# One core, two layers with gathered weights: ring blocks 2 to 7 of the first pair issued behind x, ScalarE's table loaded first, the transposes of hw in two parts, the gathers of B in four later pairs

## The reference, cut to what matters

```
def layer0(x, ids):                      # first half of the kernel
    c    = einsum('bsi,boi->bso', x, weight[ids])        # 1024x1024 adapter of each sequence
    h    = c @ lora_A.T                                  # 8 experts x rank 16
    w    = top-2 of softmax(c @ W_router.T), renormalised
    lora = 2 * sum over experts of w * (h @ lora_B.T)
    return c @ W_base.T + b_base + lora
def layer1(x, ids):                      # second half
    y = per-sequence 64x64 mix of x by weights[ids]
    return y with features permuted, 16 heads of up (64->256), gelu, down (256->64), unpermuted
x = x + layer0(x, ids);  x = x + layer1(x, ids)
```

## Time and profile before

| | |
|---|---|
| median of three runs | 613.79 us (613.06 to 614.24) |
| the profiled execution, its own time | 612.9 us |
| its span | 611.1 us, so 1.8 us lie around it |
| TensorE busy in the span | 592.6 us (97%) |
| VectorE busy | 471.5 us (77%) |
| ScalarE, GpSimd busy | 144.6 and 127.1 us |
| first phase, 18 to 276 us | TensorE busy all but 4 us of it |
| second phase, 276 to 611 us | TensorE busy 330.26 of 335 us |
| granted TensorE clock | 1.00 in every stretch |

### The profile page before, as it was taken

The page is one execution under the profiler, slowest core; times in us unless marked ns, Lnnn a source line. Parts: engine busy times, 40 slices in busy tenths (PEclk is TensorE's granted clock), DMA queues, the critical chain, the costliest instruction groups (busy, mean ns, idle before and its releaser), DMA issues.

```text
span 611.1 us, 13485 instructions
## 1 busy us (share of the span) xinstructions
PE 592.6 (97%) x4375; PEld 348.2 (57%) x4376; DVE 471.5 (77%) x1303; ACT 144.6 (24%) x290; POOL 127.1 (21%) x194
## 2 busy tenths in 40 slices
PE   4999999999998999999999999999999999999996
PEld 3344444344433444457777676767676767676762
DVE  3068778878887779698888897779987889887862
ACT  2100000200020002153332524225332235232334
POOL 4010002121111220060022222222231313131312
PEclk9999999999999999999999999999999999999999
DMA  7999889899899997120023222222222222222222
GB/s 269 409 388 316 306 307 305 308 308 315 297 409 403 352 316 254 44 69 28 19 63 94 70 90 68 88 73 88 70 86 69 88 67 94 69 86 67 88 71 86
DMA packets 43428, 106.90 MB, mean 175 GB/s; under 512 B 8451, under 2 KB 17667, under 8 KB 43395
## 3 DMA queue, kind: packets, MB, share of 16 engines
q1 hardware_dynamic: 30914, 76.04, 35.7%
q0 software_dynamic: 6784, 21.51, 10.6%
q10 hardware_dynamic: 5696, 8.95, 4.2%
HBM read 98.09 MB, written 8.39 MB: 174 GB/s over the span
## 4 chain that ended last, share of the span: by engine, by line
PE 86%; DVE 6%; DMA 4%; issue 2%; ACTq 0%; SPq 0%; POOL 0%; DVEq 0%; another core or an unknown queue 0%; POOLq 0%
PE wide L536 26%; PE bank L643 20%; PE bank L651 10%; PE bank L731 8%; PE wide L714 8%; PE y_wide L567 4%; DVE c_pair L1096 3%; DMA ring<-adapters_dram 3%; PE y_wide L689 3%; PE wide L551 2%; DMA x_in<-x_seq_dram 1%; PE bank L663 1%; PE bank L664 1%; PE bank L667 1%; PE bank L743 1%
## 5 line engine op out<-in xcount | busy, mean ns | idle before, releaser
L536 PE MATMUL wide<-ring,x_in 128*64 128x512 f32 x960 | 209.6, 592 | 2.4 <-DMA ring<-adapters_dram 2.4
L536 PEld LDWEIGHTS wide<-ring,x_in 128*64 128x64 f32 x960 | 73.1, 137 | 127.1 <-issue 127.1
L1288 DVE STREAM_TRANSPOSE x_tok<-xres 32x128 f32<-32x128 f32 x464 | 140.2, 302 | 6.0
L1096 DVE STREAM_TRANSPOSE c_pair<-wide 32x256 f32<-32x256 f32 x240 | 107.1, 446 | 39.4 <-issue 21.7
L943 ACT ACTIVATE act_sb<-wide 128x512 f32<-128x512 f32 x120 | 66.5, 610 | 191.3 <-PE wide L714 191.3
L643 PE MATMUL bank<-c_hi,base_t 128*128 128x512 f32 x384 | 102.3, 390 | 0.0
L424 POOL DMA_INDIRECT xres<-xT_dram,row_in x32 | 35.0, 1094 | 230.8 <-DVE out_sb L1278 227.6
L643 PEld LDWEIGHTS bank<-c_hi,base_t 128*128 128x128 f32 x384 | 71.9, 188 | 15.3
L651 PE MATMUL bank<-c_lo,base_t 128*128 (+1 forms) x256 | 78.0, 390 | 0.0
L462 POOL COPY c_all<-c_pair 128x512 f32 x30 | 19.3, 669 | 213.9 <-DVE c_pair L1096 213.9
L858 ACT ACTIVATE small<-small 128x1 f32<-128x1 f32 x16 | 3.2, 203 | 217.3 <-DVE small L1132 217.3
(11 more groups left out here) (161 smaller groups left out, 601.5 us busy)
## 6 DMA issues: line engine op xcount, KB each, us to landing
ring<-adapters_dram SPq DMA_DIRECT2D x128, 512.0 KB, 5.8
x_in<-x_seq_dram ACTq DMA_DIRECT2D x32, 256.0 KB, 4.8
down_sb<-down_dram SPq DMA_DIRECT2D x32, 128.0 KB
up_raw<-up_dram SPq DMA_DIRECT2D x62, 64.0 KB
ar_sb<-lora_a_router_dram ACTq DMA_DIRECT2D x1, 544.0 KB, 4.3
mix_sb<-mix_dram SPq DMA_DIRECT2D x32, 16.0 KB, 2.0
xres<-xT_dram,row_in POOLq DMA_INDIRECT x32, 3.5
out_dram<-out_sb,row_out POOLq DMA_INDIRECT x28, 3.0
```

Of the source, the lines that this page charges most:

```text
L536: last = pe.matmul(acc[half][h][z * TOK:(z + 1) * TOK, :], x_in[:, half, z, k, :], ring[:, k, z, h * HALF:(h + 1) * HALF], start=(k == 0), ...
L1096: last = nc.vector.transpose(c_pair[r * SQ:(r + 1) * SQ, :, q * SQ:(q + 1) * SQ], wide[half][q * SQ:(q + 1) * SQ, :, :] .rearrange("p h (k ...
L1288: last = nc.vector.transpose(x1_tok[q * SQ:(q + 1) * SQ, :].rearrange("p (c f) -> p c f", f=P)[:, :, f * SQ:(f + 1) * SQ], xres[f * SQ:(f ...
```

## The change

Four edits. In `first_pair` SyncE waits, ahead of block 2, until both transfers of x for pair 0 have landed. ScalarE, after it has issued its first two transfers, waits for `ident` and copies one column of it, so that its table comes in there. `turn_four` is cut: after `route` of the third pair of a batch VectorE does the 4 transposes of row block 0 of `hw`, and in the fourth pair the other 12. The gathers of B and bias go from one each in t = 4 to 11 to two each in t = 10, 11, 12 and 13 (b_rows, bias, b_rows, bias).

```
-GATHERS = range(PAIRS // 4, PAIRS // 4 + KT)
+GATHERS = {PAIRS - 6 + n: (2 * n, 2 * n + 1) for n in range(KT // 2)}
...
                 for k in range(KT):
+                    if k == 2:
+                        sp.wait_ge(x_in_in[0], 32)
                     sp.dma_start(ring[:, k, 0, :], ...)
...
-                if t in GATHERS:
-                    j = t - GATHERS[0]
+                for j in GATHERS.get(t, ()):
                     gather(b_rows[:, j, :], lora_b, perm_sb[:, j:j + 1], b_in)
                     gather(bias[:, j:j + 1], bias_rows, perm_sb[:, j:j + 1], bias_in)
...
             act.sem_inc(hw_placed, 8)
+            act.wait_ge(ident_ok, 2)
+            nc.scalar.copy(th, ident[:, 0:1])
             act.wait_ge(lists_ok, 1)
...
-            def turn_four(i):
+            def turn_four(i, qs):
-                dve.wait_ge(hw_ok, i * 4 + 4)
-                dve.wait_ge(hw_placed, i * 8 + 8)
-                for q in range(P // SQ):
+                if qs[0] == 0:
+                    dve.wait_ge(hw_ok, i * 4 + 4)
+                    dve.wait_ge(hw_placed, i * 8 + 8)
+                for q in qs:
...
-                last.then_inc(hw_turned_ok, 1)
+                if qs[-1] == P // SQ - 1:
+                    last.then_inc(hw_turned_ok, 1)
...
                     else:
-                        turn_four(i)
+                        turn_four(i, range(1, 4))
                     route(t, hw_four[:, (n + 1) % 4, :])
+                    if n == 2:
+                        turn_four(i, range(0, 1))
```

## The result

The changed kernel takes 614.99 us (median of 16 runs, 614.47 to 617.45), the kernel before 612.24 us beside it (16 runs, 611.07 to 614.24). The ratio is 1.0046 with a 95% interval of 1.0035 to 1.0056: some 2.8 us slower. The forecast said 2.1 us slower; its 615.9 was built on the earlier median of 613.79, so the sum is what can be compared. The profiled execution has a span of 613.1 us and its own time is 614.93 (before: 611.1 and 612.9); the granted clock is 0.999.

A forecast was written before the change was run, and what follows sets the result against it. TensorE is 97% busy, so only first-phase holes can move. Terms: -0.2 (x) - 0.63 (hole at t = 4) - 0.3 (ring) + 1.8 (t = 10) + 1.4 (t = 12) = +2.1 us on 613.79, giving 615.9; range 612.6 to 617.8.

The forecast's parts named there:

- the copy goes from 203.48 to 206.4: Pair 10: four gathers hold the router's signal, VectorE's copy comes late, and the next router stalls 1.8 us.
- t = 12, 1.4: Pair 12: the copy waits for the fourth gather, 2.15 us later, and the router due at 246.99 stalls 1.4 us.
- t = 13: free: Pair 13: its router starts on the spot, so the four gathers there cost nothing.
- Not t = 12 but t = 13: Rival, 0.18: router 12 escapes, router 13 is caught on the end-setting chain; 2.8 us in place of 1.4, 617.3 us.
- the rival of the slipping signal: Rival, 0.24: the signal slips out between gathers, t = 10 and 12 cost nothing; sum -1.0 us, 612.8 us.
- hw in two parts: Moving 4 of 16 transposes ahead of `turn_pair(4)` closes TensorE's hole at 119.04: 0.63 us gained.
- The gathers' going would close it too: Gathers leaving t = 4 would alone close the 0.63 us hole before router 5; not additive with the split.
- x: Start, SyncE's wait before block 2: x lands at 17.6, block 2 at 21.4; 0.2 us gained, bounds 0.5 gained, 1.9 lost.
- after block 2 the ring keeps up: Pair 0: issues 0.62 us apart and 1.3 us per block against 1.72 of matmuls, so no further waits.
- Ring bytes, -0.3: Ring-bound stretch, 163 to 190 us: two 64 KB gathers of t = 8 and 9 go, gaining 0.3 us.
- Table, 0: Start: ScalarE's table first removes TensorE's 1.13 us wait at 13.59, but nothing follows from it; 0 gained.
- two engines that share nothing but the sender: First phase: VectorE and SyncE both get TensorE's signals late during gathers; used as evidence against a port lock.

The follow-up runs named there:

- e1: The changed kernel without SyncE's wait for x: 614.29 us, ratio 1.0028.
- e2: The changed kernel with the gathers of B and bias back at t = 4 to 11, one each: 613.46 us, ratio 1.0024.
- e3: The kernel before with only the gathers moved to t = 10 to 13, two each: 612.85 us, ratio 1.0002.
- f2: The kernel before with ScalarE's table first and the gathers at t = 10 to 13, no wait for x, no split: 611.12 us, ratio 0.9983.
- e6: The kernel before with split, table first, and the old gathers waiting until VectorE has copied the router's result: 611.43 us, ratio 0.9983.
- e7: The changed kernel with the two-and-two gathers one pair earlier, at t = 9 to 12: 615.11 us, ratio 1.0031.
- e8: The changed kernel with four bias gathers each at t = 10 and 12, four b_rows gathers each at t = 11 and 13: 612.66 us, one run.
- e5: The kernel before with hw's transposes split and ScalarE's table first, old gathers, no wait for x: 613.08 us, ratio 1.0011.
- e4: The kernel before with SyncE's wait for x alone: 613.34 us, ratio 1.0024.
- f3: The kernel before with ScalarE's table first and nothing else: 612.21 us, ratio 0.9995.
- f4: The kernel before again, no edit, profiled once more: 612.94 us, one run.
- f1: The kernel before with one edit, GpSimd's gathers of B and bias waiting for VectorE's gap_ok of their pair: 611.82 us, ratio 0.9982.

## Why the prediction was right, and where its steps failed

**Sign and size: right; the mechanism behind them: right; its place: wrong.** The forecast was a loss because TensorE's signal is held while GpSimd issues several gathers in a row. e1, e2, e3 and f2 show that: the changed kernel with the old places has no such loss, and e6, with the same gathers behind the copy, has no late router's signal at all. But the step "the copy goes from 203.48 to 206.4", with its stall of 1.8 us at t = 10, failed, and so did "t = 12, 1.4". The copies came 2.1 us (t = 10), 1.7 (t = 11) and, where caught, 2.9 and 3.2 (t = 12 in f2, e7) after their router; they did not wait for the whole run, and the pair's slack took them in. (SyncE's ring issues did wait for it: 1.14 to 1.17 after the last gather, near the 0.95 of the forecast. But they had slack for it.) And the step "t = 13: free" failed the other way: 4.6 us late in the changed kernel and in e1, all of 2.8 us on the chain.

**The rival came true in its second half.** "Not t = 12 but t = 13" had the mechanism (`turn_pair(12)` behind row block 0 begins late, router 12 starts on the spot and escapes, router 13 is caught, `turn_pair(14)` at 257.0; it was 256.30) and the price: 2.8. What it also had, 1.8 at t = 10, was nothing, as in the rival of the slipping signal. Each rival held for some pairs. I had given 0.18 to the one and 0.24 to the other and none to both together. That the total came out near is luck: two forecast stalls, 3.2, stood for one real stall of 2.8 with 0.3 at router 12.

**What decides is when the router ends against the second gather's start.** GpSimd's run begins with `c_pair`; TensorE's router begins with `c_pair` too if it is late, else when the blocks are through. With four gathers in the run, by the profiles:

| run, pair | router starts behind `c_pair` | router ends, from the second gather's start | copy behind router's end |
|---|---|---|---|
| e7, t = 11 | 0.06 | 0.73 before | 0.2 |
| f2, t = 13 | 0.09 | 0.71 before | 0.7 |
| changed, t = 11 | 0.65 | 0.15 before | 1.7 |
| e7, t = 12 | 0.68 | 0.16 before | 3.2 |
| e7, t = 9 | 0.92 | 0.07 after | 1.5 |
| changed, t = 10 | 0.91 | 0.11 after | 2.1 |
| f2, t = 12 | 0.91 | 0.11 after | 2.9 |
| changed, t = 13 | 1.14 | 0.30 after | 4.6 |

A router on the spot ends in the first gather and its copy is at most 0.8 late (t = 13 in f2, e3 and e8, t = 11 in e7 and e8; at t = 12 of the changed kernel VectorE was the later). A router 0.65 us or more behind `c_pair` ends from the gap ahead of the second gather on and is caught. How late the signal then is does not follow from the table: 1.5 to 2.9 us for ends within 0.04 us of each other. So the loss takes split and new places together, which no part of the sum had: alone the new places give 1.0002 (e3), split and table 1.0011 (e5), and e1 against f2, split or no split, is 614.29 against 611.12. The split was entered as a gain of 0.63; together with the gathers it costs 3 us.

**hw in two parts, "would close the hole alone": wrong.** e5 has 16.29 at t = 4 (before: 16.22 to 16.24 in e4, f3 and f4). The step took VectorE's 1.26 us for the limit, although the row read first, the copy 0.78 after the last gather, named the other one: with transposes gone the copy still waits for the signal. "The gathers' going would close it too" was right (e3, and by f1 it is enough to move them behind the copy).

**x: the term's sign was wrong.** I counted -0.2 with bounds of -0.5 and +1.9. The part on x was near: 17.6 forecast, 17.73 measured (17.77 and 18.36 in e2 and e7), and 17.91, 18.09, 18.12, 18.34 and 18.69 in the profiles without the wait in which x was also what came last. But block 2 landed for 21.73, not 21.4, and the step "after block 2 the ring keeps up" failed: block 3 was late again by 0.52, 1.25 in e2, 0.59 in e8 (where the wait came a block further on) and 2.74 in e7. From x to pair 1 it took 15.1, 15.2, 15.3, 14.3 and 18.7 us in the five profiles with the wait, against 13.8 to 14.3 in the nine without. By the times the wait costs 0.7 (e1 against the changed kernel) to 1.5 us (e4); e2 against e5, 0.4 us, can't be told from nothing. Five of the changed kernel's 16 runs lie at 616.4 to 617.5. That they had e7's long hole with half the clock behind it is a guess and isn't shown: none of them was profiled, e7's loss at the start was 3.6 us above the changed kernel's where these runs are some 2 us above the others, and e5, without the wait, has a run at 616.38 as well. The Trainium skill's round robin by packet ("DMA: Bandwidth & Descriptors", Queues, rings and completion order), by which x would gain nothing, isn't refuted either: pair 0 started 0.4 us earlier in the first two profiles compared, but the starts with and without the wait overlap, and f4's start alone is 1.6 us off.

**Ring bytes, -0.3: not to be read from this.** The profile shows -1.31, but e4, with the old gathers, has 32.89 and f4, the kernel before, 32.54. A gain of that size can't be told from the scatter of this stretch.

**Table, 0: right** (f3).

**The sum, with what the runs gave:** x +0.9 for -0.2, t = 4 -0.63 for -0.63, ring 0 for -0.3 (the profile's -1.3 being within the scatter), t = 10 0 for +1.8, t = 12 +0.3 for +1.4, t = 13 +2.8 for 0. That adds to 3.4 for 2.1; the times show 2.8 with an interval of about 2.1 to 3.4.

**A better version.** Three kernels beat the one before, by about 1 us each by the ratios (0.7 to 1.4 by the medians), and can't be told apart: f1 (0.9982), e6 (0.9983) and f2 (0.9983). f1 adds one line, a wait. What of the change is worth having is that GpSimd's gathers don't stand beside the router; table first is harmless, split and wait for x should go.

**What stays open.** What holds the signal. Gathers of 512 bytes are enough (e8), and the ring's own traffic isn't, since that runs all the time. VectorE's signals were not held in the same stretches. At t = 11 of the changed kernel, while the last gather ran from 219.22 to 220.16, ScalarE began 0.03 us after the step of VectorE that it waits for, as it does where no gather runs:

```profile
219.88 0.16 DVE L1135 TENSOR_TENSOR small<-small 128x1 f32<-128x1 f32 x1
220.07 0.20 ACT L859 ACTIVATE small<-small 128x1 f32<-128x1 f32 x1 [14.92 <-issue]
```

SyncE is not the independent witness that the prediction took it for ("two engines that share nothing but the sender", and the argument against the port lock). At t = 13 it issues the eight transfers of `mix`, and the program makes them wait for no other engine. Before, the first is issued at 243.55 and the fifth and seventh at 248.71 and 251.19. In the changed kernel the first is issued at 243.41 and those two at 249.68 and 252.92: 1.1 and 1.9 us late, with the gathers running from 246.71 to 251.43. All five profiles with gathers at t = 13 (the changed kernel, e1, e3, e8, f2) have some of these issues late, by up to 2.2 us; the nine without have none. Timelines of SyncE's queue, 248 to 251 us, before and changed:

```profile
248.71 1.17 SPq L381 DMA_DIRECT2D mix_sb<-mix_dram  x2
```

```profile
249.68 0.00 SPq L383 DMA_DIRECT2D mix_sb<-mix_dram  x1
```

So a run of gathers also holds SyncE by itself, and its late ring issues don't prove a late signal. The lateness at VectorE does, since VectorE's own steps keep their pace. When the signal gets through is open too: 2.1, 1.7, 2.9 and 3.2 us late it came before the run's end, in the gap before the last gather or during the third or last one (203.11; 218.23; 233.77; 240.22 in e7), while at t = 13 of the changed kernel and of e1 it came 1.4 us after the last gather's end. At t = 13 no ring blocks are left to issue, and two routers ended 0.3 into the second gather rather than 0.1; I can't say whether either matters. Nor is it known why the pairs of gathers in e6 and f1 make no ring issue late. A kernel with nothing but the pairs t = 10 to 13 and a router moved in small steps against the gathers would have told it; it was not run.

## What to carry to other kernels

A wait that the profile put down to a remote or unknown releaser, while the engine that should have signalled had long ended, was a late signal here. Where you meet one, look at what a third engine issued in that time, and try moving that issue behind the wait before rearranging the work on either side. Price two edits together if one of them shifts the phase between engines: the split and the gathers each cost nothing that could be measured alone, and 3 us together. And before a few tenths at the start of a kernel are counted, profile the unchanged kernel twice: here its start and its ring-bound stretch each moved by 1.6 us with no edit at all.

## What the runs showed of the hardware that was not expected

TensorE's completion signals reached VectorE up to 4.6 us late while GpSimd issued two to four indirect gathers in a row, each 0.94 to 0.98 us with a pitch of 1.25 to 1.28, and 0.04 to 0.06 us late where no gather ran and VectorE was waiting. In the same runs of gathers SyncE's issues were late as well, those that waited for no engine included, while ScalarE acted on VectorE's signal after 0.03 us. I had read the lateness before; that it is so uneven (2.1 us and 4.6 us for the same four gathers, 0.2 us apart in phase) was new.

The Trainium skill knows one lock that ties GpSimd to another engine ("SBUF — State Buffer", Who interferes with whom) and says that TensorE and ScalarE never wait on anyone. TensorE did not wait here either, 15.59 us from router to router; what was late was the word that it had finished. No rule there would give a copy that starts 1.4 us after the last gather has ended.

The granted clock fell from 1.00 to 0.50 after TensorE had stood idle 2.74 us between two matmuls (up to 26.70, e7), and at 16 to 17 us behind 1.95 to 2.07 us of idle time (f4, e3, e6, f1; in f4 matmuls at twice their duration). It stayed at 1.00 behind e4's 2.14 us and behind e1's 2.81 us at the same place (1.09 us for the same eight), so the length of the hole alone doesn't decide. A hole at the start can cost more than its length, and not each time.
